# Projection operands on GpSimd beside the maxima, the third norm begun inside the feed-forward, and another order of work in the local attention

## The reference

```
x = x + local(ln(x))          # windows of 32 tokens, 16 heads of 16, softmax, bias on q, k, v
x = x + ffn(ln(x))            # 3 cycles: out += c * twist(out), c = 0.1 + r*2*(0.7*global + 0.3*tanh-like net(out) - 0.5)
x = x + diff(ln(x))           # differential attention over all 1024 tokens
x = x + ffn(ln(x))            # the same feed-forward once more

diff:  q = rope(x Wq), k = rope(x Wk), v = x Wv      # 32 heads of 8 for q and k, 16 heads of 16 for v
       p = softmax(q k^T / sqrt(8))
       w = p[even heads] - lambda * p[odd heads]
       y = rmsnorm(w v) * gain;  return y Wo
```

## Time and profile before

| | us |
|---|---|
| median of 3 runs (lowest to highest) | 8684.98 (8682.35 to 8692.63) |
| the profiled execution | 8688.42 |
| its span, first to last instruction | 8686.5 |
| PE busy in the span | 7654.7 (88%) |
| DVE busy | 7091.2 (82%) |
| ACT busy | 6209.5 (71%) |
| POOL busy | 3092.2 (36%) |

### The profile page before, as it was taken

One profiled execution on the slowest core, in us unless ns is written; L12 is line 12 of the kernel. 1 busy time (PEld: TensorE's weight loads), 2 busy tenths in 40 slices (PEclk: granted clock), 3 DMA queues, 4 the chain that ended last, 5 costly groups with the idle time before them and its releaser, 6 DMA issues. The chain is left out here.

```text
span 8686.5 us, 166216 instructions
## 1 busy us (share of the span) xinstructions
PE 7654.7 (88%) x65536; PEld 2784.7 (32%) x65536; DVE 7091.2 (82%) x9171; ACT 6209.5 (71%) x11506; POOL 3092.2 (36%) x4471
## 2 busy tenths in 40 slices
PE   6899978999789997899978999789997899888998
PEld 4322343223422234222342223422234222342223
DVE  5899768997689976899769997689976999769996
ACT  4599745997459974599745996559965599655996
POOL 3144231442324423244232442324423244232442
PEclk9899988999889998899998999889999899998999
DMA  0100001000010000100001000010000100001000
GB/s 29 45 20 24 15 11 45 20 24 15 11 45 21 23 15 11 45 24 20 17 9 45 24 20 20 6 45 24 21 19 6 46 23 24 19 3 48 20 24 21
DMA packets 219176, 205.43 MB, mean 24 GB/s; under 512 B 108086, under 2 KB 143414, under 8 KB 218358
## 3 DMA queue, kind: packets, MB, share of 16 engines
q1 hardware_dynamic: 218364, 194.46, 7.7%
HBM read 123.83 MB, written 67.37 MB: 22 GB/s over the span
## 5 line engine op out<-in xcount | busy, mean ns | idle before, releaser
L1299 DVE TENSOR_REDUCE mfull<-ps 128x1 f32<-128x1024 f32 x4096 | 4710.5, 1215 | 286.7 <-PE ps L1223 286.7
L1374 ACT ACTIVATE work<-ps 128x512 f32<-128x512 f32 x8192 | 4398.8, 597 | 383.1 <-PE ps L1245 264.0
L1263 PE MATMUL ps<-work,vbuf 128*32 128x256 f32 x32768 | 2623.4, 392 | 118.7 <-ACT hh L1394 118.7
L1223 PE MATMUL ps<-kop,qop 48*128 48x512 bf16 x8192 | 2548.2, 393 | 69.4 <-DVE mfull L1299 57.9
L1245 PE MATMUL ps<-qop,kop 51*128 51x512 bf16 x8192 | 2490.8, 384 | 0.0
L1263 PEld LDWEIGHTS ps<-work,vbuf 128*32 128x32 f32 x32768 | 655.9, 108 | 1762.5 <-issue 926.0
L1245 PEld LDWEIGHTS ps<-qop,kop 51*128 51x128 bf16 x8192 | 484.6, 94 | 1639.4 <-ACT work L1374 1517.5
L1325 POOL CAST mpart<-mfull 128x16 bf16<-128x16 f32 x256 | 50.4, 197 | 2608.0 <-issue 2005.9
L248 POOL TENSOR_TENSOR rstd<-rstd,nhalf 128x8 f32<-128x8 f32 x64 | 110.9, 1733 | 1629.9 <-DVE rstd L242 1629.9
L1343 POOL TENSOR_TENSOR work<-work,none 128x16 f32<-128x16 f32 x224 | 650.5, 2904 | 18.8 <-POOL mpart L1329 1.5
L440 POOL TENSOR_TENSOR hh<-work,hmask 128x1024 f32<-128x1024 f32 x256 | 521.4, 2062 | 131.6 <-PE ps L368 131.6
(11 more groups left out here) (163 smaller groups left out, 8739.4 us busy)
## 6 DMA issues: line engine op xcount, KB each, us to landing
qop<-scratch SPq DMA_DIRECT2D x512, 64.0 KB
scratch<-work SPq DMA_DIRECT2D x32, 768.0 KB, 3.6
scratch<-hh SPq DMA_DIRECT2D x32, 768.0 KB, 5.1
kop<-scratch SPq DMA_DIRECT2D x256, 96.0 KB
vbuf<-in_x SPq DMA_DIRECT2D x9, 2048.0 KB, 8.4
qop<-scratch SPq DMA_DIRECT2D x512, 32.0 KB
kop<-scratch SPq DMA_DIRECT2D x256, 64.0 KB
qop<-mT SPq DMA_DIRECT2D x1024, 3.0 KB
```

The source lines that it names most:

```text
L1223: pe.matmul(ps[:, b + n, :], qop[r:r + KQ, s, i, t * P:(t + 1) * P], kop[r:r + KQ, s, i, half(n)], start=True, stop=True).then_inc(s_ms, 1)
L1263: mm = pe.matmul(ps[VW * i:VW * (i + 1), OB, cols], vp[:, b, t, (G * gl + i) // 2, :], prob[:, u % PS, i, cols], start=t == 0 and part == ...
L1299: v.tensor_reduce(mfull[:, m // CUT % 2, r // ROWS * G // 2 + i, to:to + 1], ps[:, b:b + NB, :].rearrange("p b n -> p (b n)"), AX.X, ALU.m ...
L1374: act.activation(prob[:, u % PS, hl, :], ps[:, EB[slot % len(EB)], :], ACT.Exp, scale=scale).then_inc(s_ex, 1)
```

## The change

Three things are changed.

1. Local attention. The v pieces of sequence 0 move from ahead of the loop into passes 0 and 1; all pieces of sequence 1 come two passes later. All regrouping, residuals and `spread` come behind the loop. ACT's `keep` comes ahead of `place`. `values` waits for its own piece of v only.
2. Norm n3. For sequence 0 it is made inside f1: POOL makes -mean*rstd, ACT the normalised tiles and all four copies of the transposes, and PE goes on with unit 0 of the projection. The block of n3 keeps sequence 1.
3. Projection. DVE multiplies one half of a unit at a time. For units 0 and 1 DVE still takes c = 0 and POOL c = 1; all six steps of units 2 and 3 are POOL's, while DVE goes on to the maxima. PE projects v of sequence 1 between the first 16 score tiles. SP loads the q operands of group 0 behind unit 0, those of k behind unit 1, groups 1 and 2 next, then writes units 2 and 3 and waits for them, and only then issues the maxima.

```
@@ layernorm
+        def norm_turned(pe, t, s_h, s_tp):        # the transposes of tile t, as before
+            s_h, s_tp = ahead[0:2] if ahead else (sem(f"{tag}_{n}") for n in ("h", "tp"))
+            N0 = NB if ahead else 0
-                    for n in range(CH + 1):
+                    for n in range(N0, CH + 1):
@@ local_attention, tensor
-                        if tb == 0:
-                            pe.wait_ge(s_vz, VR * (b + 1))
+                        pe.wait_ge(s_vz, VR * b + tb // 2 + 1)
-                    for r in range(VR):
-                        v_piece(0, r)
                     for t in range(TT + 2):
...
-                        if t < 4:
-                            qk_piece(1, t)
-                        elif t < 8:
-                            v_piece(1, t - 4)
-                        if REGROUP <= t < REGROUP + 4:
-                            regroup(0, t - REGROUP)
-                    for k in range(4):
-                        regroup(1, k)
+                        if t < 2:
+                            v_piece(0, 2 * t)
+                            v_piece(0, 2 * t + 1)
+                        elif t < 6:
+                            qk_piece(1, t - 2)
+                        elif t < 10:
+                            v_piece(1, t - 6)
+                    for b in range(PB):
+                        for k in range(4):
+                            regroup(b, k)
@@ local_attention, vector (v_keep(0, .) at t < 2 and v_keep(1, .) at 7 <= t < 11, behind turn)
-                        if REGROUP < t <= REGROUP + 4:
-                            residual(0, t - REGROUP - 1)
-                        if t == REGROUP + 4:
-                            spread(v, norm, 0)
+                    for k in range(4):
+                        residual(0, k)
+                    spread(v, norm, 0)
@@ local_attention, scalar
+                        if t >= 3:
+                            keep(t - 3)
                         if 1 <= t <= TT:
                             place(t - 1)
-                        if t >= 3:
-                            keep(t - 3)
-                        if t < 4:
-                            qk_keep(1, t)
+                        if 2 <= t < 6:
+                            qk_keep(1, t - 2)
@@ ffn, tensor, at the end
+                        pe.wait_ge(s_tz, NB)
+                        for t in range(T):
+                            norm_turned(pe, t, s_h, s_tp)
+                        pe.wait_ge(s_ln, C * NB)
+                        first_unit(pe)
@@ ffn, scalar, at the end
+                        act.wait_ge(s_nb, 2)
+                        for t in range(T):
+                            act.activation(h[:, t, :], x[:, t, :], ACT.Identity, bias=nb[:, t:t + 1],
+                                           scale=rstd[:, t:t + 1]).then_inc(s_h, 1)
+                        for n in range(NB):
+                            act.wait_ge(s_tp, 4 * (n + 1))
+                            for c in range(C):
+                                act.copy(hT[:, 0, c, half(n)], ps[:, c * NB + n, :]).then_inc(s_ln, 1)
@@ ffn, gpsimd, at the end
+                        pool.tensor_scalar(nb[:, :], mv[:, 0:T, 0], -1.0, None, ALU.mult).then_inc(s_nb, 1)
+                        pool.wait_ge(s_nb, 1)
+                        pool.tensor_tensor(nb[:, :], nb[:, :], rstd[:, 0:T], ALU.mult).then_inc(s_nb, 1)
@@ diff_project, vector (multiply(i, m) makes the two products of bank pair m)
+                for i in range(UNITS):
+                    shared = 1 <= i <= BY_BOTH
+                    multiply(i, 0)
+                    if shared:
+                        remainder(v, i - 1, 0)
+                    multiply(i, 1)
+                    if shared:
                         last_part(v, i - 1, 0)
-                    if i < UNITS:
+                    if i < BY_BOTH:
                         rotated(v, i, 1)
                         rotated(v, i, 0)
@@ diff_project, gpsimd
-                for i in range(UNITS):
+                for i in range(BY_BOTH):
                     remainder(pool, i, 1)
                     last_part(pool, i, 1)
+                pool.wait_ge(s_c3[0], BY_BOTH)
+                for i in range(BY_BOTH, UNITS):
+                    for step in (rotated, remainder, last_part):
+                        for c in range(2):
+                            step(pool, i, c)
@@ diff_project, scalar
+                    if i == BY_BOTH:
+                        kept(0)                    # between the two pairs of casts of unit 2
@@ diff_attention, sync
-                    for g in range(SLOTS):
-                        operands(g)
+                    operands(0, (0,))
                     project_sp(sp, 1)
                     projected_sp(sp, 1)
+                    operands(0, (1,))
+                    for g in range(1, SLOTS):
+                        operands(g)
+                    for i in (2, 3):
+                        project_sp(sp, i)
+                        projected_sp(sp, i)
                     maxima(0)
@@ diff_attention, tensor (value_tile: one tile of v of sequence 1 ahead of score tiles 1, 3, ..., 15)
                     for e in CLOCK:
+                        if value_tile(e) is not None:
+                            project_values(pe, value_tile(e))
@@ main loop
+            n3_ahead = [sem(f"n3_{n}") for n in ("h", "tp", "nb", "ln")]
+            project = diff_project()
+            ffn("f1", n3, ahead=n3_ahead, first_unit=lambda pe: project[0](pe, first_unit=True))
+            layernorm("n3", n3, ahead=n3_ahead)
+            diff_attention(*project)
```

More of the change, by code:

```diff
@@ L104, in build @@
         rstd = sb("rstd", [P, TT])
+        nb = sb("nb", [P, T])
         nhalf = sb("nhalf", [P, TT])
@@ L282, in _ @@
                 def _(pe):
[L283 to L289, removed]
+                    for t in range(4 * N0, TT):
+                        norm_turned(pe, t, s_h, s_tp)
                 @block.scalar
                 def _(act):
-                    for n in range(CH):
+                    for n in range(N0, CH):
                         b, cols = chunk_of(n)
@@ L746, in _ @@
                     last(Z)
+                    if ahead:
+                        s_h, s_tp, s_nb, s_ln = ahead
+                        act.wait_ge(s_nb, 2)
[4 more added lines that the diff above has]
+                            act.wait_ge(s_tp, 4 * (n + 1))
+                            for c in range(C):
+                                act.copy(hT[:, 0, c, half(n)], ps[:, c * NB + n, :]).then_inc(s_ln, 1)
                 @block.vector
@@ L914, in projected, with project_values @@
                         mm.then_inc(s_pj, 1)
[L916 to L921, removed]
-                                           wv[:, c, :], start=c == 0, stop=c == C - 1)
-                        mm.then_inc(s_vj, 1)
-                for i in range(UNITS):
+                if first_unit:
+                    projected(0)
+                    return
+                for i in range(1, UNITS):
                     projected(i)
-                for b in range(PB):
-                    values(b)
+                pe.wait_ge(s_rm, 4 * (UNITS - 1))
+                for t in range(T):
+                    project_values(pe, t)
                 pe.wait_ge(s_ve, T // 2)
+            def project_values(pe, i):
+                b, t = i // T, i % T
+                if i == T:
+                    pe.wait_ge(s_rm, 4 * UNITS)
+                for c in range(C):
+                    mm = pe.matmul(ps[:, 4 * b + t // 2, (t % 2) * D:(t % 2 + 1) * D],
+                                   hT[:, b, c, t * P:(t + 1) * P],
+                                   wv[:, c, :], start=c == 0, stop=c == C - 1)
+                mm.then_inc(s_vj, 1)
             def rotated(eng, i, c):
@@ L986, in project_act @@
                 for i in range(UNITS):
-                    for c in (1, 0):
+                    order = (1, 0) if i < BY_BOTH else (0, 1)
+                    for c in order:
                         act.wait_ge(s_ra[c], i + 1)
@@ L991, in project_act @@
                         act.copy(part[i % 2][:, c, 0, :], turned[i % 2][c]).then_inc(s_c1[c], 1)
-                    for c in (1, 0):
+                    if i == BY_BOTH:
+                        kept(0)
+                    for c in order:
                         act.wait_ge(s_r1[c], i + 1)
                         act.copy(part[i % 2][:, c, 1, :], rest[i % 2][c]).then_inc(s_c2[c], 1)
-                        if i == UNITS - 2 and c == 1:
-                            kept(0)
                 kept(1)
@@ L1151, in max_bank, with value_tile @@
                 return 2 * (m % 2)
+            def value_tile(e):
+                i = e + AHEAD
+                return T + i // 2 if i % 2 == 1 and 0 <= i < 2 * T else None
             def turn_at(h):
@@ L1175, in _, with operands @@
                 def _(sp):
-                    def operands(g):
```

(1 more changed line is left out.)

70 lines of the change are left out of this document (37 added, 33 removed).

## The result

| | before | after |
|---|---|---|
| median, 4 runs each (lowest to highest) | 8685.45 (8682.35 to 8692.63) | 8544.85 (8536.97 to 8556.34) |
| the profiled execution (its span) | 8688.42 (8686.5) | 8556.34 (8554.7) |
| mean granted clock of PE | 0.944 | 0.954 |

The ratio of after to before is 0.9838, 95% interval 0.9821 to 0.9855: 140.6 us faster, where 8530 was forecast. (The kernel before ran again beside it, hence its four runs.) The two profiled executions lie 132.1 us apart.

The account below looks back on a forecast made before the run. DVE's reductions of the maxima were taken to set the pace while the attention runs. An earlier first reduction (18.4) plus local attention (1.1) made 19.5 us a pair, 156 for eight: 8530 us, range 8475 to 8610.

Parts of the forecast that it names:

- The stretch from M to R: Projection, DVE's first product (M) to its first reduction of the maxima (R): 32.3 us forecast, against 49.1 before.
- R to E: DVE's first reduction (R) to PE's first exponential tile (E): claimed to stay 26.4 us.
- The rule of the Trainium skill: DVE beside POOL: port lock only for two SBUF inputs or 2-port mode, never `tensor_reduce`; reductions lose nothing.
- The rival of POOL being late: First `cut`, behind twelve POOL operations: at double their length exponentials start 5.6 us later, 8720; chance 0.03.
- The n3 step: Norm n3, partly moved inside f1: DVE's first product 1.6 us earlier, bounds 4 earlier and 3 later.
- Start: Local attention, up to the first maximum: 5.6 us earlier, at 2229.3 against 2234.95.
- the passes: Local attention's loop, from first to last maximum: 0.5 us shorter a pair.
- the tail: Local attention behind the loop: -2.7 us as `place(15)` waits less, +7.7 for four more regroup pieces.
- the forecast's groups: Local attention passes by kind: 9.3 us for two v pieces, 24.1 four q/k, 20.05 four v, 21.4 five plain.
- the term for the lower clock (+3): Local attention's plain passes: PE thinly loaded, at 1.2 GHz, costs 3 us, some 0.85 for each of the last four.
- What `keep` ahead of `place` gives (-2.5): Local attention: `keep` leaves the loop that spans two passes, 0.37 us less in two, -2.5 in all.
- The prediction's mirror rival: Local attention: the passes drop to ACT's 3.6 us, gain 25 a pair, 8485; chance 0.11.

Follow-up runs that it names:

- all_shared: The changed kernel with POOL and DVE sharing all four projection units, as before the change: 8654.65 us.
- v_ahead: The changed kernel with the v tiles of sequence 1 in one row ahead of the maxima, as before the change: 8584.1 us.
- pool_late: The changed kernel with two more POOL operations of the same kind ahead of its unit 3, their results overwritten: 8573.32 us.
- n3_undone: The changed kernel with norm n3 behind f1 for both sequences and unit 0 back in the projection, as before: 8578.78 us.
- filler: The changed kernel with four more matmuls, whose result nothing reads, in each of passes 11 to 15 of the local attention: 8499.64 us.
- unit0_back: The changed kernel with only unit 0 put back at the head of the projection, n3 of sequence 0 staying in f1: 8551.26 us.
- warm_passes: warm_gaps with idle products also ahead of values in pass 11 (three) and pass 13 (one): 8473.09 us.
- warm_all: warm_gaps with three more idle products ahead of either half of n3's transposes: 8525.04 us.
- warm_gaps: regroup_inside with idle products on PE, two ahead of values(14) and four ahead of the last third cycle of both feed-forwards: 8473.72 us.
- regroup_inside: The changed kernel with the regrouping of sequence 0 back in passes 11 to 14 of the local attention: 8488.27 us.

## Why the prediction was right

**The stretch from M to R: right in size and cause.** Forecast 32.3, measured 32.4 in the third pair and 32.7 in the mean. Its inner steps held too: k loads issued at M+27.4 (forecast 27.8) and the first score tile at M+31.8 (31.5). all_shared and v_ahead show by taking away that this is the eight operations off DVE (10.5 of the 16.4 a pair) and the v tiles out of the way (4.3). In whole time they cost 110 and 39 us, together more than the gain, because all_shared also lengthens R to E by 5.0.

**R to E unchanged: right**, 26.6 against 26.4. POOL was done at M+49.1 (49.8 forecast), though its gap before the cut was 2.4 and not close to nothing, because the first cut came 0.4 later than forecast and POOL's end 0.7 earlier. The reductions beside POOL took 1218 ns, those without it 1216. The rule of the Trainium skill (SBUF — State Buffer, "Who interferes with whom") held where it decided. Its other half is in the traces as well: DVE's `remainder`, two SBUF inputs, takes 1.21 alone at 2433.07 and 2.11 beside POOL in all_shared. The rival of POOL being late lay 1.2 us away, by pool_late.

**The n3 step: right in kind, half in size.** The forecast was 1.6 earlier, measured 0.8. Eight normalised tiles took 4.05 (4.0 taken) and the copies 2.00 (2.2). What was mis-sized is the added "1.0" for unit 0 at the lower clock, which was 1.5 (8.63 against 7.1), so that PE closed f1's block 4.4 us behind DVE, and small waits in n3, 0.4. By n3_undone the whole step is worth 34 us all the same, part of it behind M.

**The local attention: the start right, the rest off by compensating sizes.** Start -5.6 as forecast. In the mean the passes came out at +1.5 in place of -0.5, the tail at +4.0 in place of +5.0: -0.1 in place of -1.1 together. In the third pair the passes took 78.4, and the forecast's groups, which add up to 74.9 less 2.5 and plus 3, make 75.4. Two terms failed. Passes 0 and 1, with two v pieces each, took 10.44 in place of 9.3, in every pair. And the term for the lower clock (+3) was for the plain passes alone: they lost 3.8 by filler, and a v piece at the lower clock (3.42) made the four v passes 1.6 longer (20.71, against 19.07 in the first pair, where it ran at full clock). What `keep` ahead of `place` gives (-2.5) was not tried by itself; that the v passes at full clock and the four before them came out some 1.0 and 0.5 shorter than their terms agrees with it. How often the clock falls was luck as far as the forecast goes: the same passes took 73.8 in five pairs of unit0_back.

**The sum** was 19.5 a pair and came out at 16.5: 1.0 of the difference lies in the local attention, 0.8 ahead of M, 0.4 in M to R, 0.2 at R to E, and the rest in stages that were taken as unchanged. The prediction's mirror rival, gains of the passes, was not the change's but one edit away: with regrouping inside the loop the time is 8488, within 3 us of the 8485 that the mirror gave. That is a coincidence: it came by another way (a short tail, not passes at ACT's pace).

## What to carry to other kernels

Work in the idle gaps of a loop is not paid in full: four pieces of necessary work inside the loop, in gaps in which PE's granted clock fell to 0.50 without them, cost 2 to 3 us, and the same pieces behind it 7.3 us. When operations are taken off the engine that paces, follow the data they feed through its DMAs first: here their way through DRAM, not DVE, closed the new stretch. And look for the second gate beside the one that the profile names before believing its idle time to be slack.

## What was not expected of the hardware

- The same code takes one of a few lengths from pair to pair: the passes in the new order 73.8, 76.0 or 78.4 us, among others, f1 93.8, 95.5 or 96.5, f2 93.15, 94.85 or 95.3. In the passes filler shows that this is PE's granted clock falling to 1.2 GHz. An edit elsewhere changes which length comes, and may hide 16 of 22 us (unit0_back) or give a gain back (warm_passes). An edit's worth is then better read from its own stages than from the whole time.
- Adding matmuls that nobody needs made the kernel 45 us faster in one place (filler) and 51 us slower in another (warm_all against warm_gaps).
- What decides which pair falls to the lower clock and where stays open: no run here separates it. So does whether the 15 us between regroup_inside and warm_gaps are real.
